# Spectral products of a Fourier layer stack on one core: one operand copy goes to GpSimd, one eviction to VectorE

## The reference

```python
for l in range(LAYERS):
    sc = _spectral_conv(h, w1r[l] + 1j * w1i[l], w2r[l] + 1j * w2i[l])   # rfft2, products, irfft2
    pw = jnp.einsum('bihw,oi->bohw', h, pw_w[l]) + pw_b[l][None, :, None, None]
    y = sc + pw
    ...                                                                   # batch norm, gelu
# in _spectral_conv: 16 x 16 modes at the top and as many at the bottom of the spectrum
top = jnp.einsum('bixy,ioxy->boxy', xf[:, :, :M1, :M2], w1)
bot = jnp.einsum('bixy,ioxy->boxy', xf[:, :, -M1:, :M2], w2)
```

## Time and profile before

| | us |
|---|---|
| median of three runs | 2551.52 (2549.45 to 2554.74) |
| profiled execution, its time | 2540.21 |
| profiled execution, its span | 2538.4 |
| the four `mix` stages, from ACT's first L646 to the end of its last L654 | 52.26, 52.00, 51.98, 52.09 |

### The profile page before, as it was taken

The page is one execution under the profiler, slowest core; times in us unless marked ns, Lnnn a source line. Parts: engine busy times, 40 slices in busy tenths (PEclk is TensorE's granted clock), DMA queues, the critical chain, the costliest instruction groups (busy, mean ns, idle before and its releaser), DMA issues. The chain is left out here.

```text
span 2538.4 us, 79362 instructions
## 1 busy us (share of the span) xinstructions
PE 2173.8 (86%) x34571; PEld 1444.8 (57%) x34571; DVE 1648.9 (65%) x2562; ACT 1667.6 (66%) x2640; POOL 152.2 (6%) x172
## 2 busy tenths in 40 slices
PE   7779989976997998599979966996999599964999
PEld 4657757755665776566657755664222355552444
DVE  4868878884777887577778884776000576754444
ACT  1924468875776787767778875775999466641433
POOL 0000000000000000000000000000000022201443
PEclk9989989998999999899989998998999699976999
DMA  5656657658996873899957658997653100012433
GB/s 184 227 179 240 235 209 264 211 186 267 370 372 230 293 263 137 267 319 377 367 215 263 210 197 278 363 375 283 231 178 95 36 2 2 2 28 55 105 84 74
DMA packets 175734, 524.91 MB, mean 207 GB/s; under 512 B 22879, under 2 KB 37951, under 8 KB 175167
## 3 DMA queue, kind: packets, MB, share of 16 engines
q1 hardware_dynamic: 175391, 519.84, 60.1%
HBM read 350.02 MB, written 170.37 MB: 205 GB/s over the span
## 5 line engine op out<-in xcount | busy, mean ns | idle before, releaser
L416 PE MATMUL P<-cst,mem 128*128 128x128 f32 (+1 forms) x3760 | 502.2, 283 | 53.0 <-ACT mem L709 13.9
L675 ACT ACTIVATE mem<-P,small 128x512 f32<-128x512 f32 x512 | 309.8, 688 | 310.1 <-PE P L524 249.3
L416 PEld LDWEIGHTS P<-cst,mem 128*128 128x128 f32 (+1 forms) x3760 | 415.9, 144 | 161.5 <-issue 126.2
L832 DVE BATCH_NORM_STATS2 mem<-mem 128x6 f32<-128x512 f32 x512 | 315.2, 678 | 5.7 <-ACT mem L675 5.7
L870 DVE COPY mem<-P 128x512 f32<-128x512 f32 x384 | 248.0, 686 | 99.8 <-PE P L416 98.4
L524 PEld LDWEIGHTS P<-cst,mem 64*128 64x128 f32 (+1 forms) x5120 | 239.2, 166 | 95.9 <-issue 95.7
L524 PE MATMUL P<-cst,mem 64*128 64x128 f32 (+1 forms) x5120 | 260.4, 275 | 0.0
L665 ACT ACTIVATE mem<-mem,small 128x1024 f32<-128x1024 f32 x192 | 229.1, 1250 | 39.4 <-DMA mem<-z_d 39.4
L825 DVE COPY mem<-P 128x512 f32<-128x512 f32 x256 | 165.0, 686 | 127.5 <-PE P L501 127.5
L820 DVE COPY mem<-P 128x512 f32<-128x512 f32 x256 | 165.4, 686 | 119.9 <-PE P L416 119.9
L709 ACT ACTIVATE mem<-mem,small 128x1024 f32<-128x1024 f32 x192 | 232.8, 1248 | 6.3 <-DMA mem<-z_d 5.3
(11 more groups left out here) (164 smaller groups left out, 2936.3 us busy)
## 6 DMA issues: line engine op xcount, KB each, us to landing
mem<-z_d SPq DMA_DIRECT2D x360, 512.0 KB, 5.1
z_d<-mem SPq DMA_DIRECT2D x256, 512.0 KB, 6.9
mem<-in_wmix SPq DMA_DIRECT2D x64, 1024.0 KB, 8.6
G_d<-mem SPq DMA_DIRECT2D x128, 256.0 KB, 4.0
mem<-G_d SPq DMA_DIRECT2D x128, 256.0 KB, 7.6
hz<-z_d SPq DMA_DIRECT2D x64, 512.0 KB, 4.3
mdB<-dT_d SPq DMA_DIRECT2D x44, 384.0 KB, 5.7
mem<-in_x SPq DMA_DIRECT2D x128, 12.0 KB
```

Of the source, the lines that this page charges most:

```text
L416: return nc.tensor.matmul(out, in_, ident[0:n, 0:n], start=True, stop=True, is_transpose=True)
L675: nc.scalar.activation(ychunk(l, a, h), P[4 + 2 * (a.q % 2) + h][:, :], ACT.Identity, bias=bias0 if first else pwb_c).then_inc(S["eY"], 1)
L832: nc.vector.bn_stats(so, ychunk(l, a, h)).then_inc(S["eS"], 1)
```

## The change

GpSimd gets the plain copy (v=0) of every step, with a semaphore `sgP` of its own. DVE keeps the negated half and takes the eviction of each step's second bank from ACT, in the order three negations ahead, then per step eviction and the negation for step s+3. ACT keeps its copy and the first eviction. The load of the first images counts on `s_const` instead of a semaphore of its own, which makes room for `sgP`; its waiters wait for 48 there.

```diff
+            def mix(l):
+                if l == 0:
+                    enter(pool, "pool", 1)
+                else:
+                    pool.wait_ge(S["eXd"], l * 16)
+                    pool.wait_ge(S["eXa"], l * 16)
+                for s in range(MSTEPS):
+                    if s >= 3:
+                        pool.wait_ge(S["pM"], l * 32 + 2 * s - 4)
+                    nc.gpsimd.tensor_copy(operands(s)[:, 0], spectra(s)).then_inc(S["sgP"], 1)
+                leave(pool, "pool")
...
-                    pe.wait_ge(S["sgD"], l * 32 + 2 * s + 2)
+                    pe.wait_ge(S["sgD"], l * 16 + s + 1)
+                    pe.wait_ge(S["sgP"], l * 16 + s + 1)
                     pe.wait_ge(S["sgA"], l * 16 + s + 1)
...
                     nc.scalar.activation(Gs[s % 4][:, 0:512], P[2 * s % 8][:, :], ACT.Copy).then_inc(S["eMd"], 1)
-                    act.wait_ge(S["pM"], l * 32 + 2 * s + 2)
-                    nc.scalar.activation(Gs[s % 4][:, 512:1024], P[(2 * s + 1) % 8][:, :], ACT.Copy).then_inc(S["eMa"], 1)
                     if s + 3 < MSTEPS:
                         stage(s + 3)
...
                     nc.vector.tensor_scalar(operands(s)[0:64, 1], spectra(s)[64:128], -1.0, None, ALU.mult).then_inc(S["sgD"], 1)
-                    nc.vector.tensor_copy(operands(s)[:, 0], spectra(s)).then_inc(S["sgD"], 1)
+                for s in range(3):
+                    stage(s)
                 for s in range(MSTEPS):
-                    stage(s)
+                    dve.wait_ge(S["pM"], l * 32 + 2 * s + 2)
+                    wait(dve, gst[s % 4], l * 128 + 32 * (s // 4) if s >= 4 else 0)
+                    nc.vector.tensor_copy(Gs[s % 4][:, 512:1024], P[(2 * s + 1) % 8][:, :]).then_inc(S["eMa"], 1)
+                    if s + 3 < MSTEPS:
+                        stage(s + 3)
```

More of the change, by code:

```diff
@@ L157, in build_fno @@
             "s_const", "w_loaded", "z_zero", "sp_phase", "s_zero", "s_w0", "s_parload",
-            "a0_pe", "a0_ev", "a0_mx", "a0_re", "a0_im", "sgA", "sgD",
+            "a0_pe", "a0_ev", "a0_mx", "a0_re", "a0_im", "sgA", "sgD", "sgP",
             "z_gelu", "pT1", "pF1", "pT2", "pF2", "pX", "eT1", "eF1", "eT2", "eF2", "eXd", "eXa",
@@ L162, in build_fno @@
             "pe_phase", "act_phase", "dve_phase", "pool_phase", "chain", "pStat", "eStat", "sAggr", "sVar", "sRstd",
-            "x0_load", "kept_st")}
+            "kept_st")}
         zl = [[sem(f"zl{u}{q}") for q in range(4)] for u in range(2)]
@@ L265, in _ @@
             sp.dma_start(cst[:, NEARLY:], consts[:, NEARLY:]).then_inc(S["s_const"], 16)
-            sp.dma_start(xall, x6.rearrange("b p n -> (b p) n")).then_inc(S["x0_load"], 16)
+            sp.dma_start(xall, x6.rearrange("b p n -> (b p) n")).then_inc(S["s_const"], 16)
             for w in range(0, W_EARLY, 2):
@@ L402, in _ @@
             leave(pool, "pool")
-            for n in range(1, 2 * layers + 1):
-                enter(pool, "pool", n)
+            def mix(l):
[9 more added lines that the diff above has]
+                leave(pool, "pool")
+            for l in range(layers):
+                if l:
+                    enter(pool, "pool", 2 * l + 1)
+                mix(l)
+                enter(pool, "pool", 2 * l + 2)
                 leave(pool, "pool")
@@ L409, in _ @@
         def _(pe):
-            pe.wait_ge(S["s_const"], 32)
-            pe.wait_ge(S["x0_load"], 16)
+            pe.wait_ge(S["s_const"], 48)
             def tr(out, in_):
@@ L753, in link @@
                 dve.wait_ge(S["chain"], chained[0])
-            dve.wait_ge(S["s_const"], 32)
+            dve.wait_ge(S["s_const"], 48)
             for n, (kind, g, h) in enumerate(A0):
```

## The result

| | kernel before | changed kernel |
|---|---|---|
| median, first comparison | 2552.95 us (2549.45 to 2554.74, 4 runs) | 2574.98 us (2570.71 to 2582.38, 4 runs) |
| median, second comparison, later | 2540.9 us (12 runs) | 2568.17 us (2566.71 to 2569.14, 4 runs) |
| the four `mix` stages in the profile | 52.26, 52.00, 51.98, 52.09 | 62.36, 58.75, 58.07, 62.27 |

What follows compares the result with a forecast made beforehand. POOL with DVE was to bound `mix`: copy 2.17 plus negation hold 1.12 is 3.29 us per step; 16 x 3.29 + 2.85 = 55.5 against 52.1, four times, +14 on 2551.5: 2566 us, range 2518 to 2606 (forecast's own 2548 to 2588).

Steps and rivals of the forecast that it cites:

- exclusion: In `mix`, DVE's negation and POOL's copy shut each other out: 2.17 + 1.12 = 3.29 us per step; chance 0.40.
- near rivals: In `mix`: ACT still the bound, chance 0.33, 2525 us; exclusion with a dearer POOL copy, chance 0.22, 2596 to 2635 us.
- What bounds the kernel, and what ACT wins: In `mix`, ACT is busy 205.3 of 208.3 us; losing one eviction saves it 0.49 us per step.
- The price of the copy: POOL's strided copy in `mix` takes 2.17 us: 1.29 contiguous plus 0.88 for the stride; ends 0.9 and 3.27.
- the estimate of 2.65 us: POOL's copy by the page's 2.9 cycles with the fixed part: `mix` 63.2 us, total 2596; dearer copies' chance 0.22.
- The prediction's growth of 0.5 us per step: What the page's 2.9 cycles per element for POOL's copy, given as 2.47 us, would add to each `mix` step.
- The sum: One `mix` is 16 x 3.29 + 2.85 = 55.5 us against 52.1: +3.4 us, four times, +14 us.
- Edits at nothing: In `mix`, DVE's eviction waiting for stores, POOL's added phases and the merged load semaphore cost nothing.
- The signs to look for: In `mix`: PE starts just behind POOL copies, POOL's and DVE's staging never overlap, ACT has half-microsecond gaps per step.
- One sign: A `mix` of 60 us and more would mean the mechanism holds and the POOL copy was priced too cheap.
- ACT as the bound: In `mix`, no exclusion or a POOL copy of 1.66 us or less: 45.4 us per stage, total 2525; chance 0.33.
- a microsecond or two: Store waits in `mix`, with parameter loads in SP's queue, take this per layer from the ACT-bound rival's gain.

Runs made afterwards that it cites:

- the other form: Changed kernel with DVE's negation written as tensor_reduce, a sum over one element with negation: 2528.5 us against 2549.1 before, ratio 0.9917.
- in turns: Changed kernel with one more wait, POOL's copy of step s waiting for DVE's negation of step s-1: 2553.0 us against 2541.9 before, ratio 1.0033.
- the gather part alone: Kernel before with the plain copy moved to POOL, DVE only negating, both evictions staying on ACT: 2565.2 us against 2541.9 before, ratio 1.0071.

## Why the prediction was right

It gave 2566 us and a slower kernel by 14 us; the first comparison gave 22, the second 27. The sign and the mechanism, exclusion, were right; the size fell short, and the reason lies in one step. It was foreseen with a chance of 0.40 and no more, so the single number was a choice between near rivals.

*What bounds the kernel, and what ACT wins.* Borne out. ACT's busy time fell by 25.2 us in four stages; 64 evictions at 0.49 us are 31.4, and its copies became longer (2.23 us on average, 2.15 before). That the end of `mix` is carried through one for one agrees with the 2325 to 2339 us outside the stages in all profiles.

*The price of the copy.* I took 2.17 us; in runs of three it is 2.14. That is partly luck: the contiguous part was 1.04 where I had 1.29, and the stride 1.1 where I had 0.88. The two errors cancel. The 2.9 cycles per element by the page "GPSIMD Engine Reference" of the Trainium skill (Performance pitfalls for Q7 kernels), from which the estimate of 2.65 us came, are too many here: 2.14 us are 2.5 cycles per element at its 1.2 GHz, with any fixed part still in them. The prediction's growth of 0.5 us per step belongs to these 2.65 us; with its 2.47 it would be 0.3.

*The exclusion.* Shown by the pair of runs that differ in the form of the negation alone, 240.9 against 203.8 us, and by the ends of the held negations, in the changed kernel always 0.95 to 1.12 us behind a copy's end. What is shown is which instructions exclude each other. That the cause is one shared way into SBUF is an inference: the other form is also slower by itself, and no run here has a slow negation that is held up, or a fast one that runs beside a copy. The rule of the page "SBUF — State Buffer" of the Trainium skill (Who interferes with whom), that VectorE's two-port mode and GpSimd exclude each other and that `tensor_reduce` on this chip doesn't take part, agrees with both.

*The sum, 16 x (2.17 + 1.12) + 2.85.* This is the step that failed. It lets the two take turns, one negation per copy. Where that was enforced the sum holds: 54.4 us per stage against my 55.5, +11 us against my +14. Left to themselves, POOL runs several copies in a row, and the term of 3.29 us per step should have been 3.68 in a round of three, and 3.59 on average over the four stages, (241.45 / 4 - 2.85) / 16. The round of three is made of 6.4 for the copies, 1.0 for the negation behind them, 3.6 for PE's step at the lowered clock, before POOL may start again. The clock was not in my sum at all. The hold of a single negation was priced well, 1.12 us against 0.95 to 1.12. Of what is measured beyond the turns, 241.5 - 217.7 = 23.8 us in the profiles, I can't say how much is the clock and how much the longer wait; no run separates them.

*Edits at nothing.* The waits for stores came to 8.7 us on ACT and 0.3 on DVE in all four stages, mostly while other waits were longer. No run tells whether they cost something there.

*The signs to look for.* ACT had gaps, 61.3 us in 64 steps, about 1 us where I gave half a one, and the two staging instructions showed the wide spread. But that PE's steps would start just behind a POOL copy was wrong: 44 waits of PE and its weight loads ended with the negation and 2 with the copy. I took the longer of the two for the later one; in a run the copy comes first and the negation last. One sign misleads: stages of 60 us and more were to mean that the copy was priced too cheap, and two of the four last 62 us with a copy of 2.14, less than its price.

*The rivals.* ACT as the bound was one property away. With the same kernel and the other form of the negation a stage lasts 48.6 us on average; my 45.4 for that rival was too low by 3.2. ACT's load was priced well, 2.76 us of busy time per step against my 2.78. But its evictions waited 10.8 us in all for stores, 2.7 per layer, where I gave a microsecond or two; that this makes up the difference is likely and not shown, since DVE is as full as ACT there.

## What to carry to other kernels

Before work moves to POOL, ask not only how long it takes there but which of DVE's remaining instructions read and write SBUF in the fast one-input mode. Where both engines stage operands, as here, these run one behind the other, and whichever engine is in goes on with all of its instructions that stand ready before the other gets a turn: three or four copies before a negation, three negations before a copy. Two cheap remedies were measured here: a semaphore that makes them take turns (took away some two thirds of the loss), and a slower DVE form outside that mode (turned a loss of 1% into a gain of 0.8%). An engine's busy share tells of none of this, since an instruction that is held up counts as busy; its minimum and maximum do, and the median not always (1.31 us in the gather part alone, beside a maximum of 10.1).

## What the runs showed that I had not expected

- A DVE instruction of 0.21 us took 6.17 us behind three POOL copies. The hold-up is not one instruction long but a run. It holds for DVE's runs too: a POOL copy of 1.04 us took 4.3 us at the start of a stage, behind three negations.
- Making one instruction slower (1.31 to 2.16 us in the median, 64 times) made the gather part 37 us faster in the sum of the stages. With the time held up counted, the mean went down, from 3.01 to 2.21.
- POOL's contiguous copy of 128x1024 took 1.04 us; DVE's strided one took 1.39 on average. The source step doubles POOL's time to 2.14.
- After PE had idled 3.5 us, its next 3.6 us ran at a granted clock of 0.55, and the stages of the changed kernel had 0.75 to 0.85 on average, against 0.92 to 0.97 in turns.
